# A fused attention and feed-forward layer on one core: VectorE turns tile 7 a step earlier, GpSimd makes three of its splits later, TensorE turns tile 0 after the projections

## The reference

```
q = (x @ Wq) in heads;  k, v = halves of (x @ Wkv) in heads        # 16 heads of 64
s = q @ k^T / 8                                                   # per head 1024 x 1024
gm = max of s over each whole row (before masking)
p = where(upper triangle, 0, exp(s - gm))
out = (p @ v) / (sum(p) + 1e-8)
x1 = layernorm(x + concat(out) @ Wo + bo)
prev = x1 shifted by one token
r = sigmoid((mu_r*x1 + (1-mu_r)*prev) @ W_r^T);  k = (mu_k*x1 + (1-mu_k)*prev) @ W_k^T
result = layernorm(x1 + r * (relu(k)^2 @ W_v^T))
```

## Time and profile before

| | |
|---|---|
| time, median of 3 runs | 1112.6 us (1112.58 to 1112.87) |
| the profiled execution's own time | 1111.76 us |
| its span | 1110.0 us |
| TensorE busy | 1037.7 us (93%) |
| VectorE busy | 914.9 us (82%) |
| ScalarE busy | 748.0 us (67%) |
| GpSimd busy | 579.4 us (52%) |
| mean share of the DMA queue SP uses | 50.6% |

### The profile page before, as it was taken

One profiled execution on the slowest core, in us unless ns is written; L12 is line 12 of the kernel. 1 busy time (PEld: TensorE's weight loads), 2 busy tenths in 40 slices (PEclk: granted clock), 3 DMA queues, 4 the chain that ended last, 5 costly groups with the idle time before them and its releaser, 6 DMA issues. The chain is left out here.

```text
span 1110.0 us, 22041 instructions
## 1 busy us (share of the span) xinstructions
PE 1037.7 (93%) x7427; PEld 676.6 (61%) x7427; DVE 914.9 (82%) x1546; ACT 748.0 (67%) x1706; POOL 579.4 (52%) x918
## 2 busy tenths in 40 slices
PE   7799999999999999999999999999999999999684
PEld 5565666666656666666666666666666666666363
DVE  5888888988887888888877988888888888889564
ACT  5666666666676676666766666666667666676475
POOL 5355655555556555565564555556655556563233
PEclk9999999999999999999999999999999999999698
DMA  5245565545555645455555454555565445555601
GB/s 159 72 111 124 124 143 135 122 108 123 125 120 130 143 121 122 117 117 131 129 126 137 112 123 112 126 133 125 136 143 125 114 120 117 130 128 128 144 19 57
DMA packets 74193, 134.05 MB, mean 121 GB/s; under 512 B 26849, under 2 KB 36833, under 8 KB 74081
## 3 DMA queue, kind: packets, MB, share of 16 engines
q1 hardware_dynamic: 73504, 132.26, 50.6%
q10 hardware_dynamic: 576, 0.39, 0.1%
HBM read 21.17 MB, written 2.36 MB: 21 GB/s over the span
## 5 line engine op out<-in xcount | busy, mean ns | idle before, releaser
L679 DVE TENSOR_SCALAR_CACHE_REDUCE tile<-ps_s 128x1024 f32<-128x1024 f32 x512 | 608.1, 1222 | 137.9 <-PE ps_s L872 132.7
L535 ACT ACTIVATE tile<-tile,neg_max 128x640 f32<-128x640 f32 (+7 forms) x512 | 396.2, 774 | 211.0 <-POOL tile L383 210.8
L872 PE MATMUL ps_s<-ks,qs 64*128 64x512 f32 x3072 | 425.5, 409 | 10.1 <-DVE tile L679 8.3
L383 POOL TENSOR_SCALAR_AFFINE_SELECT tile<-tile 128x128 f32<-128x128 f32 x512 | 149.5, 293 | 455.6 <-DVE tile L679 453.5
L872 PEld LDWEIGHTS ps_s<-ks,qs 64*128 64x128 f32 x3072 | 269.6, 185 | 129.1 <-issue 61.1
L926 PE MATMUL ps_x<-pt,vs 128*64 128x256 f32 (+1 forms) x2560 | 270.2, 362 | 0.0
L688 DVE STREAM_TRANSPOSE stage<-tile 128x640 f32<-128x640 f32 (+3 forms) x256 | 255.0, 1025 | 0.0
L926 PEld LDWEIGHTS ps_x<-pt,vs 128*64 128x64 f32 x2560 | 173.1, 137 | 108.2 <-issue 34.2
L885 PE MATMUL ps_x<-ident,tile 128*128 128x128 f32 x640 | 117.1, 290 | 26.3 <-ACT pt L583 15.6
L885 PEld LDWEIGHTS ps_x<-ident,tile 128*128 128x128 f32 x640 | 69.0, 140 | 106.7 <-issue 51.7
L806 PE MATMUL ps_x<-xs,ws 128*128 128x512 f32 x381 | 119.0, 421 | 0.6 <-DVE xs L654 0.5
(11 more groups left out here) (83 smaller groups left out, 576.2 us busy)
## 6 DMA issues: line engine op xcount, KB each, us to landing
pt<-stage SPq DMA_DIRECT2D x512, 120.0 KB, 2.4
pt<-stage SPq DMA_DIRECT2D x512, 88.0 KB, 2.1
rb<-recips SPq DMA_DIRECT2D x64, 256.0 KB, 4.1
out<-y SPq DMA_DIRECT2D x4, 512.0 KB, 3.2
y<-in_L_attn_x SPq DMA_DIRECT2D x3, 512.0 KB, 8.3
pt<-in_L_attn_Wkv SPq DMA_DIRECT2D x2, 384.0 KB, 6.6
pt<-in_L_attn_x SPq DMA_DIRECT2D x2, 256.0 KB, 4.5
wos<-in_L_attn_Wo SPq DMA_DIRECT2D x1, 512.0 KB, 7.1
```

The lines of the kernel that those rows point to most:

```text
L383: pool.affine_select(out=block_of, in_=block_of, compare_op=ALU.is_ge, fill=fill, base=0, pattern=[[-1, P]], channel_multiplier=1).then_in ...
L535: act.activation(cols, cols, ACT.Exp, bias=neg_max[:, at:at + 1], scale=-1.0, accum_out=sums[:, p % 2, a, t:t + 1]).then_inc(s_exp, 1)
L679: dve.tensor_scalar(tile[:, at, :], ps_s[scores_at(p, t, a)][:, :], -SCALE, None, ALU.mult, ALU.min, accum_out=neg_max[:, at:at + 1]).then ...
L872: ins = mm(ps_s[scores_at(p, t, a)][:, c * HALF:(c + 1) * HALF], qs[rows, p % 2, qh, t * P:(t + 1) * P], ks[rows, p % 2, kh, c * HALF:(c + ...
```

## The change

Three tables of numbers and one piece of VectorE's list are altered; no instruction is added or removed.

- `SPLIT_AT`: in which step GpSimd makes which split. The first stays in step 0, the other three go from steps 2, 4, 5 to steps 4, 5, 6, each behind the second mask of its step.
- `TURN_FIRST`: in the steps listed, the turn by TensorE comes ahead of the projections. Step 1 is taken out: tile 0 is turned behind the value and q/k projection of step 1; with it the order of the banks and of ScalarE's copies changes.
- VectorE turns tile 7 of the pair before between the two evacuations of step 0 (head 0) and behind the second of step 1 (head 1), instead of behind the second of step 1 and between the two of step 2. The two small instructions of the reciprocals go from behind step 0 to between the two evacuations of step 1.

```diff
-SPLIT_AT = {0: 0, 2: 1, 4: 2, 5: 3}
+SPLIT_AT = {0: 0, 4: 1, 5: 2, 6: 3}
 V_AT = {0: 0, 1: 1}
 TURN_AT = {1: 0, 2: 1, 3: 2, 4: 3}
-TURN_FIRST = (1, 3, 4)
+TURN_FIRST = (3, 4)
...
                     evacuate(p, t, 0)
-                    if t == 2 and p > 0:
-                        turn_tile(p - 1, TILES - 1, 1)
+                    if t == 0 and p > 0:
+                        turn_tile(p - 1, TILES - 1, 0)
+                    if t == 1 and p > 0:
+                        recips_of(p - 1)
                     evacuate(p, t, 1)
-                    if t == 0 and p > 0:
-                        recips_of(p - 1)
                     if t == X_AT:
                         for b, c in x_half(p):
                             low_of_tokens(b, c)
                     if t == 1 and p > 0:
-                        turn_tile(p - 1, TILES - 1, 0)
+                        turn_tile(p - 1, TILES - 1, 1)
```

## The result

The changed kernel takes 1154.3 us (median of 4 runs, 1148.7 to 1156.1), the kernel before 1112.6: a ratio of 1.037, 95% interval 1.033 to 1.041. It is slower by 41.7 us, where +5.4 was forecast: the direction held, the size did not, and the time lies outside the range of 1109 to 1127.

A forecast was written before the change was run, and what follows sets the result against it. TensorE was taken as the bound: 24 ordinary pairs at +0.40 us (+9.6) and six with tokens at -0.70 (-4.2) make +5.4 on 1112.6, so 1118.0 us, own range 1115 to 1122, overall 1109 to 1127.

The forecast's parts named there:

- TensorE as the bound: TensorE busy 30.76 of 31.43 us in pair 16; changes elsewhere count only where they move a wait of TensorE.
- the chain of step 1: Later evacuation, GpSimd's row and ScalarE's copies delay tile 1's turn; scores of step 3 come 0.94 us late.
- an ordinary pair: Pair without tokens, 24 in the sum: +0.40 us each, with +0.25 to +0.55 from rounding.
- a pair with tokens: Six pairs where tokens are also turned: -0.70 us each, bounded by -1.3 and 0.
- VectorE: VectorE's list: nothing added; second evacuation of step 0 goes 1.28 us later, reciprocals take some 0.6 us in step 1.
- The late reciprocals: Rival, chance 0.08: spreading DMAs land too late for GpSimd's norm of step 3; at worst 0.65 us a pair, 1134 us.
- The margin of 0.15 us: At the median landing time of 4.1 us, the reciprocals' DMAs reach the norm of step 3 in time by 0.15 us.
- The sum's price for late reciprocals: At a landing time of 4.9 us, 0.65 us in each of 24 pairs, +15.6 us.
- Splits at nothing: GpSimd's three later splits, in steps 4, 5 and 6, were reckoned to cost nothing.
- What comes back in step 3: Masks no longer wait for a split and TensorE's wait at tile 2's second turn goes: 0.4 to 0.5 us.
- The rival on the other side: ScalarE's copy of the step-2 projection does not hold tile 1's turn: -0.10 us an ordinary pair, 1106.0 us, chance 0.12.
- the one on the order of DMAs: Skill rule: one ring's descriptors go in order, so only six moves ahead could delay the spread; lowered that rival's chance a little.

The follow-up runs named there:

- `a_accum`: The changed kernel with L694, the small addition before the reciprocals, in the form that also writes an accumulator: 1120.7 us, 1.0074.

## Why the prediction was wrong

- **TensorE as the bound, and the chain of step 1** (evacuation, split, mask, norm, mask, exponential, copy, bank): right in kind, and closer in its sum than in its parts. With the reciprocals back in step 0, an ordinary pair costs 0.38 us more (forecast 0.40), a pair with tokens 0.88 less (0.70), the kernel 4.0 more (5.4). Part of that nearness is luck. In pair 15 of that kernel the scores of step 3 come 0.76 us late (11.46 us after those of step 0, before 10.70), where 0.94 was forecast, mostly because a turn of tile 7 ahead of an evacuation costs 1.16 us and not 1.28. Step 3 then gives back 0.36 (3.26 against 3.62), where 0.44 was forecast, and step 4 gives back 0.01, where 0.10 was forecast.
- **VectorE**: the step that failed. "The reciprocals some 0.6 us with their gap" (529.3 less 528.7; 1.51 us in the changed kernel, 545.29 to 546.80) took L694's 0.17 from a place where no long GpSimd instruction ran. Between the evacuations of step 1 it runs beside the split's subtraction and takes 1.24. I had written down that the split runs from about 527.9 to 529.9 and the reciprocals from 528.7, and did not lay the two beside each other. On VectorE alone it costs little: the kernel with the hold and the shorter DMA chain is at 1115.8. What it costs goes by the DMAs of the reciprocals to the norm of step 3 and from there to TensorE.
- **The late reciprocals**: named as a rival at 0.08, with 1134 us as its dear end. Its chain was right link by link: forecast for the second issue 534.03, found 534.97, and the 0.94 between them is the hold less what came earlier ahead of it. Its sign, a wait of L391 for this DMA, is what the trace shows. The margin of 0.15 us was far too thin to give it 0.08: of the hold's 1.07 us next to nothing is covered. And a wait for two DMAs ends with the slower one, which the median of 4.1 over single DMAs flatters: the slower of the two has a median of 4.4, and pair 16 had 5.2. With that the margin is gone even without the hold, as `a_accum` shows, where the norm still waits (17.7 us, of which 6.8 at the end).
- **The sum's price for late reciprocals** was capped at 0.65 us a pair by the greatest landing time of before, and put on 24 pairs; in the changed kernel the norm waits in 31, with a median of 1.32 us and up to 3.4, with a landing of 6.4. That TensorE's granted clock can fall after such a wait, some 4.7 us here, was in no term of the sum.
- **Splits at nothing**: right; alone they change nothing (1111.8). **What comes back in step 3**: right in an ordinary pair (above), where the wait for L583 is gone. Pair 16, by whose clock I had reckoned, is one of two in the run where it stays (0.23 us), so its step 3 lasts 3.55 us (553.90 less 550.35) against 3.62; why, no run tells.
- **The rival on the other side** did not occur: the wait of tile 1's turn for L543, which would have had to be absent, is in the list, though only half as long as forecast.

The Trainium skill states the hold in "SBUF — State Buffer", section "Who interferes with whom": a VectorE operation in a two-port mode, which a `tensor_scalar` can enter except in the form that also writes out its accumulator, and a GpSimd operation lock each other out for a whole instruction. The runs agree: 1.24 us plain, 0.17 us with the accumulator, beside the same instruction. That L694 runs in such a mode is inferred from this, no row names it. Had I weighed this rule instead of the one on the order of DMAs, L694 would have been priced at up to the 1.27 us of a subtraction, and late reciprocals would have become the forecast, at about 0.95 us a pair (1.27 less 0.17, less the margin of 0.15). On the 24 ordinary pairs that is an estimate of 1141 us, nearer to 1154.3 but still short of it.

## What to carry to other kernels

A small instruction has to be priced by what runs beside it in its new place on another engine (here GpSimd's subtraction), not by its duration in the old one; and a result that leaves by DMA has to be followed to its last user with that price in it. Where the margin at the end of such a chain is smaller than the spread of one link, it is no margin. Where three waits end within a tenth of a microsecond of each other, moving one of them gains nothing: find how long the step must last for each before taking any away.

## What the hardware showed that I had not expected

- `TENSOR_SCALAR` fp32 128x16 on VectorE beside a GpSimd `TENSOR_TENSOR` 128x512: 1.24 us, ending 0.02 us after it (median over the run 1.24). Started 0.07 us ahead of it, in pair 28: 0.17. Started later beside the same instruction, with the reciprocals alone moved, the median was 0.36. `RECIPROCAL` of the same shape was at 0.25 us in every run, also beside GpSimd's mask and norm, and the `STREAM_TRANSPOSE` of 128x1024 at 1.24, beside the norm and beside a split's `CAST`.
- TensorE was granted half its clock after three waits of 1.54 to 3.35 us in the midst of the run, about 1.6 us lost each time.
- An evacuation that follows a turn without a wait starts 1.16 us after it (541.87 to 543.03), not 1.28 as I had read from a place with a small gap.
- The spreading DMAs of 256 KB landed 3.5 to 6.4 us after issue in the changed kernel, 3.6 to 4.9 before.
